# Smaller pieces for the quantising pass over three weights, two PSUM banks instead of four in the attention groups, and waits moved to the buffers now used

## The reference, cut to what matters

```
sa, ca, ga, sb, cb, gb = split(silu(c) @ wmod)            # ga, gb: at least 0.25 in size
h = layernorm(x) * (1 + ca) + sa
x = x + ga * attn_block(h)      # q, k, v, attention over the 16 heads of a token, o, gelu MLP 1024-4096-1024
h = layernorm(x) * (1 + cb) + sb
x = x + gb * ffn(h)

def weight_quant(w): s = 1 / clip(mean(|w|), 1e-5); return clip(round(w * s), -1, 1) / s
def act_quant(x):    s = 127 / clip(max(|x|, rows), 1e-5); return clip(round(x * s), -128, 127) / s
def bitlinear(x, w): return act_quant(x) @ weight_quant(w).T
def ffn(x): return bitlinear(silu(bitlinear(x, w_gate)) * bitlinear(x, w_up), w_down)
```

## Time and profile before

| | us |
|---|---|
| median of 2 runs | 8587.61 (8584.29 and 8590.92) |
| the profiled execution, its own time | 8546.85 |
| its span (first to last instruction, slowest core, core 7) | 8545.1 |
| spans of the 8 cores | 8489.9 to 8545.1 |
| outside the span in that execution | 1.75 |
| core 7, from the start to the first load of pass 1 | 412 |
| core 7, the three weights' preparation | 412 to 1037 |
| core 7, the eight chunks | 1037 to 8545 |

### The profile page before, as it was taken

The page is one execution under the profiler, slowest core; times in us unless marked ns, Lnnn a source line. Parts: engine busy times, 40 slices in busy tenths (PEclk is TensorE's granted clock), DMA queues, the critical chain, the costliest instruction groups (busy, mean ns, idle before and its releaser), DMA issues.

```text
span 8545.1 us, 71718 instructions; the slowest of 8 cores (8489.9 to 8545.1 us)
## 1 busy us (share of the span) xinstructions
PE 4842.0 (57%) x23948; PEld 2382.1 (28%) x23948; DVE 3130.7 (37%) x5728; ACT 1002.1 (12%) x2077; POOL 73.6 (1%) x109
## 2 busy tenths in 40 slices
PE   0700066666565575665666666656566656656566
PEld 0700033223322152223322242224322332224222
DVE  0033343253315432354325432543335331543244
ACT  0000011111111011101111111101110111111110
POOL 0011000000000000000000000000000000000000
PEclk9999966887688776886688767877788768867788
DMA  9555501333032311332033212341133203321133
GB/s 106 146 201 202 200 30 35 74 84 94 22 79 68 89 50 30 78 90 69 23 79 86 79 41 56 76 104 36 34 74 85 88 22 80 74 81 51 37 80 89
DMA packets 1033748, 667.50 MB, mean 78 GB/s; under 512 B 806192, under 2 KB 937392, under 8 KB 1017264
## 3 DMA queue, kind: packets, MB, share of 16 engines
q1 hardware_dynamic: 1018608, 537.09, 24.2%
q0 software_dynamic: 14784, 125.84, 6.1%
HBM read 646.09 MB, written 67.11 MB: 83 GB/s over the span
## 4 chain that ended last, share of the span: by engine, by line
PE 41%; DMA 23%; DVE 19%; issue 9%; ACT 5%; another core or an unknown queue 3%; DVEq 1%; ACTq 0%; SPq 0%; POOL 0%; POOLq 0%
PE pA L586 5%; PE pB L586 4%; PE pB L1066 4%; DMA wbigB<-scr_u 3%; DMA wbigB<-scr_fc 3%; DVE sbd L678 3%; PE pA L1060 3%; DVE vtmp L1150 2%; DMA wbigA<-scr_u 2%; PE pB L933 2%; DVE vtmp L489 2%; PE bcA L264 2%; DMA wbigB<-scr_g 2%; PE pA L933 2%
## 5 line engine op out<-in xcount | busy, mean ns | idle before, releaser
L942 DVE SCALAR_TENSOR_TENSOR vtmp<-pA,c_projb_f,afm 128x512 f32<-128x512 f32 x32 | 24.0, 751 | 1047.4 <-PE pA L933 1047.4
L439 PE MATMUL bcA<-amid,onescol_b 128*1 128x512 bf16 x256 | 99.3, 557 | 471.6 <-DVE amid L432 471.6
L1082 DVE TENSOR_TENSOR gu<-pB,gt 128x512 f32<-128x512 f32 x256 | 177.0, 692 | 453.7 <-PE pB L1066 453.7
L1060 PE MATMUL pA<-mmin,wbigB 128*128 128x512 bf16 x1024 | 258.0, 391 | 136.4 <-DMA wbigB<-scr_g 94.5
L1060 PE MATMUL pA<-mmin,wbigA 128*128 128x512 bf16 x1024 | 260.7, 394 | 117.6 <-DMA wbigA<-scr_g 73.6
L264 PE MATMUL bcA<-siluc,gfm 128*128 128x1 f32 x768 | 164.1, 352 | 247.7 <-DMA gfm<-wmod 247.7
L1066 PE MATMUL pB<-mmin,wbigB 128*128 128x512 bf16 x1024 | 253.5, 392 | 89.3 <-DMA wbigB<-scr_u 89.0
L1080 ACT ACTIVATE sig<-gt 128x512 bf16<-128x512 f32 x256 | 161.5, 631 | 1142.6 <-DVE gt L1077 1142.5
L1066 PE MATMUL pB<-mmin,wbigA 128*128 128x512 bf16 x1024 | 253.3, 392 | 58.0 <-DMA wbigA<-scr_u 57.3
L350 PE MATMUL bcB<-onecol_f,trA 128*1 128x1 f32 x6 | 0.6, 163 | 491.0 <-DVE prep_r L339 491.0
L586 PE MATMUL pA<-mmin,wbigA 128*64 128x256 bf16 x1536 | 225.3, 290 | 38.9 <-ACT mmin L499 38.9
(11 more groups left out here) (266 smaller groups left out, 8697.1 us busy)
## 6 DMA issues: line engine op xcount, KB each, us to landing
gfm<-gB POOLq DMA_DIRECT2D x32, 1024.0 KB, 6.2
gfm<-uB POOLq DMA_DIRECT2D x32, 1024.0 KB, 6.3
gfm<-dB POOLq DMA_DIRECT2D x32, 1024.0 KB, 6.2
wbigB<-scr_fc SPq DMA_DIRECT2D x128, 256.0 KB, 2.9
wbigA<-scr_fc SPq DMA_DIRECT2D x128, 256.0 KB, 2.9
wbigB<-scr_g SPq DMA_DIRECT2D x128, 256.0 KB, 2.9
wbigA<-scr_u SPq DMA_DIRECT2D x128, 256.0 KB, 2.8
wbigA<-scr_g SPq DMA_DIRECT2D x128, 256.0 KB, 2.9
```

Of the source, the lines that this page charges most:

```text
L1060: ev_mg = p.op("tensor", (lambda oc, kc, wbg_, slg: lambda t: t.matmul(out=pslot(slg), lhsT=wbg_[:, kc * 128:(kc + 1) * 128], rhs=mmin[:, ...
L1082: ev_p3 = p.op("vector", (lambda slu, gt, gu: lambda v: v.tensor_tensor(out=gu[:], in0=pslot(slu), in1=gt[:], op=ALU.mult))(slu, gt, gu), ...
```

## The change

Three things are changed.

1. Pass 2 of `prep_quant` works in pieces. Each tile is still loaded whole (1 MB, by POOL, two buffers). VectorE takes it in four pieces of 512 columns: piece h is multiplied and rounded into its own int32 buffer `prep_iv[h]` (trA, rsxg_t, sxb2_t, scaleb_t, which the chunks use later) and clipped into half of a bf16 buffer `prep_bv[h // 2]` (the two gt tensors). After pieces 1 and 3 SP stores 128 x 1024 bf16 (256 KB). The clip of a piece also waits for the last store from its buffer (`st_last`). The multiply waits for `evo`, which is reassigned at each store.
2. The attention's groups use midA and midB in turn (g mod 2) instead of four banks.
3. Since gfm's first half is no longer used by the preparation, Gelu's outputs 0 to 15 of chunk 0 no longer wait for the last store of the preparation, and 16 to 31 still do. The first users in chunk 0 of trA, rsxg_t, sxb2_t, scaleb_t and of the two gt tensors in the gate stage wait for that store.

```diff
@@ prep_quant, pass 2
-                evi = p.op("vector", (lambda buf, sw_col: lambda v: v.tensor_scalar(
-                    out=prep_i[:], in0=buf[:], scalar1=swb[:, sw_col:sw_col + 1],
-                    scalar2=None, op0=ALU.mult))(buf, sw_col),
-                    deps=(evd, ev_swb, evo), sig=True)
-                evc = p.op("vector", lambda v: v.tensor_scalar(
-                    out=prep_b[:], in0=prep_i[:], scalar1=1.0, scalar2=-1.0,
-                    op0=ALU.min, op1=ALU.max), deps=(evi,), sig=True)
-                evo = p.op("sync", (lambda r, c0: lambda s: s.dma_start(
-                    out=dst[128 * r:128 * (r + 1), c0:c0 + 2048], in_=prep_b[:]))(r, c0),
-                    deps=(evc,), dma="q")
+                for h in range(4):
+                    evi = p.op("vector", (lambda buf, sw_col, h: lambda v: v.tensor_scalar(
+                        out=prep_iv[h], in0=buf[:, 512 * h:512 * (h + 1)],
+                        scalar1=swb[:, sw_col:sw_col + 1],
+                        scalar2=None, op0=ALU.mult))(buf, sw_col, h),
+                        deps=(evd, ev_swb, evo), sig=True)
+                    evc = p.op("vector", (lambda h: lambda v: v.tensor_scalar(
+                        out=prep_bv[h // 2][:, 512 * (h % 2):512 * (h % 2) + 512],
+                        in0=prep_iv[h], scalar1=1.0, scalar2=-1.0,
+                        op0=ALU.min, op1=ALU.max))(h),
+                        deps=(evi, st_last[h // 2]), sig=True)
+                    if h % 2 == 1:
+                        evo = p.op("sync", (lambda r, c0, h: lambda s: s.dma_start(
+                            out=dst[128 * r:128 * (r + 1),
+                                    c0 + 1024 * (h // 2):c0 + 1024 * (h // 2) + 1024],
+                            in_=prep_bv[h // 2][:]))(r, c0, h),
+                            deps=(evc,), dma="q")
+                        st_last[h // 2] = evo
                 evq_hist.append(evo)
@@ attention, per group
-                mname = mname4[g % 4]
-                mb = midp4[g % 4]
-                vb = vst_ps4[g % 4]
+                mname = "mid%d" % (g % 2)
+                mb = midp[g % 2]
+                vb = vst_ps[g % 2]
@@ Gelu of chunk 0
-                deps=[ev_mm] + ev_const + ([prep_done["d"]] if ci == 0 else []), sig=True)
+                deps=[ev_mm] + ev_const +
+                ([prep_done["d"]] if (ci == 0 and oc >= 16) else []), sig=True)
```

More of the change, by code:

```diff
@@ L203, in build_nc @@
     prep_r = sb("prep_r", [128, 18])
+    prep_iv = [trA[:, :].bitcast(I32), rsxg_t[:, :].bitcast(I32),
+               sxb2_t[:, :].bitcast(I32), scaleb_t[:, :].bitcast(I32)]
+    prep_bv = [gtr[0][:, :].bitcast(BF16), gtr[1][:, :].bitcast(BF16)]
     pP = [psal("pA", [128, 1024]), psal("pB", [128, 1024])]
@@ L208, in build_nc @@
     vst_ps = [midp[0][:, 264:296].bitcast(BF16), midp[1][:, 264:296].bitcast(BF16)]
-    midp4 = None
     sems = {s: ctx.enter_context(nc.semaphore(s)) for s in
             ("sT", "sV", "sS", "sG", "sQ", "dq0", "dq1", "dg0", "dg1")}
-    midp4 = [midp[0], midp[1], bcp[0], bcp[1]]
-    vst_ps4 = [mb_[:, 264:296].bitcast(BF16) for mb_ in midp4]
-    mname4 = ["mid0", "mid1", "bc0", "bc1"]
     BT = {"bc0": [], "bc1": [], "mid0": [], "mid1": []}
@@ L371, in prep_quant @@
         evq_hist = []
+        st_last = [None, None]
         i = 0
@@ L978, in build_nc @@
                     out=trA[:], in0=hfm[:, 0:chunk], in1=hfm[:, chunk:2 * chunk],
-                    op=ALU.max), deps=[evs_h2[0], evs_h2[1], evs_h2[-1]] +
+                    op=ALU.max), deps=[evs_h2[0], evs_h2[1], evs_h2[-1],
+                                       prep_done["d"] if ci == 0 else None] +
                     ([("dq0", p.counts["dq0"]), ("dq1", p.counts["dq1"])] if DBG else []),
@@ L1011, in build_nc @@
             out=rsxg_t[:], in_=bcp[1][:, 0:chunk], func=AF.Identity),
-            deps=(ev_rgb,), sig=True)
+            deps=(ev_rgb, prep_done["d"] if ci == 0 else None), sig=True)
         bank_r("bc1", ev_rgt)
@@ L1076, in build_nc @@
                 dep_p1.append(ev_prod[-2])
+            if ci == 0 and oc < 2:
+                dep_p1.append(prep_done["d"])
             ev_p1 = p.op("vector", (lambda slg, gt: lambda v: v.tensor_tensor(
@@ L1124, in build_nc @@
             out=sxb2_t[:], in_=bcp[0][:, 0:chunk], func=AF.Identity),
-            deps=(ev_sxb2,), sig=True)
+            deps=(ev_sxb2, prep_done["d"] if ci == 0 else None), sig=True)
         bank_r("bc0", ev_sxt2)
@@ L1141, in build_nc @@
             out=scaleb_t[:], in_=bcp[1][:, 0:chunk], func=AF.Identity),
-            deps=(ev_scb,), sig=True)
+            deps=(ev_scb, prep_done["d"] if ci == 0 else None), sig=True)
         bank_r("bc1", ev_sct)
```

## The result

The changed kernel takes 8748.7 us (median of 11 runs), the kernel before 8586.62 (median of 10). The ratio is 1.0184, with a 95% interval from 1.0149 to 1.0218: 158 us or 1.8% slower, where 8730 and 1.7% were forecast. The ratio leaves out one run of the changed kernel in which the four cores of one die were slower at a lower clock. The profiled execution took 8725.05 us.

A forecast was written before the change was run, and what follows sets the result against it. Pass 2 of the weight preparation was seen as a ring waiting for stores; 42 longer rounds (124.7 us) plus first and last tiles made 142.7 us, so 8587.6 + 142.7 = 8730 us, range 8615 to 8800.

The forecast's parts named there:

- The ring: Pass 2 of the preparation: a round holds two stores in sequence, 11.11 us, 2.97 more than 8.14, in 42 rounds: 124.7 us.
- The stores: Pass 2: a tile's first store stands behind the load, 4.7 us; the second finds no load, 1.95 us.
- VectorE: Pass 2 pieces: multiply 486 ns, clip 427 ns, a half tile 2.05 us, a tile 4.10 where it was 2.62.
- The cover: Pass 2: VectorE's longer work counts in full in each round, 4.10 us a tile where it was 2.62.
- Banks and moved waits: Attention's two banks (1.97 us of slack) and Gelu's and chunk 0's moved waits: both costed at nothing.
- Rival 1: Pass 2: the first store gets out ahead of the load, both stores cost 1.95 us, 8615 us; chance 0.13.
- Rival 2: Pass 2: stores cost by number, not size, 5.3 and 2.65 us, a round of 12.41, 8793 us; chance 0.19.
- Rival 3: Pass 2: not slower; smaller stores slip past the load at 1.6 us each, round 7.66, 8577 us; chance 0.04.
- rival 4: Attention: a wait for the bank at each group, 51 us on top of the forecast, 8781 us; chance 0.02.

The follow-up runs named there:

- the two partial kernels: Changed kernel with old pass 2 put back: 0.998 of the kernel before; changed kernel with four attention banks again: 1.0196 of the kernel before.

## Why the prediction was right

- The ring. The step said that pass 2 is a ring of multiply, clip and store, and that the reassigned `evo` puts two stores into it. Taking away the wait of piece 2 alone gives back 153.2 of 154.1 us. Shown.
- The stores. The first behind the load was put at 4.7 us, with 5.17 if the load does not move forward. The rows give 233.5 us of waiting for 48 first stores; six of them (first and last tiles) wait about 2.2, which leaves 5.24 for each of the other 42, and less the hand-overs of 0.18 a landing of 5.06. The term was mis-sized by 0.36 us in 42 rounds, 15 us. The second was put at 1.95; 106.6 us over 45 waits (125.8 less 19.2 for loads) are 2.37, or 2.19 for the store, 11 us more over all rounds. In all VectorE waits 359 us ahead of its multiplies, for the 333 forecast.
- VectorE. 486 and 427 ns to the nanosecond (480 and 481 for the multiplies of pieces 1 and 3). A half tile takes 1.95 us and not 2.05, since the second multiply starts 0.1 us before the first clip's end (497.16 for 496.81 + 0.43): 0.1 us in each of 96 half tiles, some 10 us less. Together 142.7 + 15 + 11 - 10 = 159, beside 154 on average and 156 between the two cores whose rows are used (1193.3 on core 3 now, 1037.1 on core 7 before). The errors partly cancel.
- The cover. I let VectorE's extra time count in full, 1.5 us a round. With one store a tile it would not have counted at all; the four pieces alone are even faster than the whole tile. In the changed kernel the first half's work is hidden as well: the first store lands 7.1 us into the round, where half of the old store's data would have landed at 7.3. The loss is what stands behind that landing: the second half tile, 1.95 us, its store, 2.2, and two hand-overs. Much of the 0.36 us above is this same thing, counted from the store's issue.
- Banks and moved waits at nothing. Shown by the two partial kernels; the groups of the attention start 2.4 to 2.8 us apart before and now.
- Rival 1 (the first store gets out ahead) did not come about, and its reasoning was wrong as well: it compared the bulk of the load's data, 3.0 us into the round, with the store's at 2.85. The row itself has the load's first data at 2.0 to 2.2 us and full flow from 3.2, and the kernel with the load after the multiply shows that a thin flow between them is of no use to a store issued behind the load. The load's issue, 0.45 us into the round, is always ahead of a store at 2.03. The rule of the Trainium skill that I leaned this rival on (SBUF — State Buffer, Who interferes with whom: the two engines block each other) agrees with POOL's rows, an issue of 527 ns alone and 690 now, but the load never came late enough. Rival 2 (cost by number) is refuted as the cause: the second store takes 2.2 us and not 2.65, and with the wait of piece 2 gone the number of stores costs 25 us. Rival 3 did not come about, and rival 4 is refuted by the partial kernels.

## What to carry to other kernels

Before splitting a transfer into smaller ones, look at what the producer waits for: an event variable that is reassigned inside the new loop made each half wait for the other, and the overlap that the second buffer allows was never used. Where one transfer sets the length of a ring, see whose turn it is in the DMA queues. A prefetch whose issue began 0.9 us ahead of the store on the critical path made that store 4 us longer (6.7 for 2.7), and letting the load wait for the clip, in place of the store's landing, bought 101 us in one line. Also look at which operation a wait protects: the store reads what the clip writes, so it is the clip that has to wait for it, and not the multiply.

## What the runs showed of the hardware that I had not expected

- A store of SP that was issued while POOL was still issuing a load moved nothing for 3.2 us, although hardly anything flowed in 0.9 of them; then both flowed beside each other for about 1.6 us. Issued 0.5 us ahead of the load it landed in 2.7 us. What holds it is not shown.
- The load's own length is not the same in all kernels, at the same 1 MB. Median of pass 2, from issue to landing: 5.2 us with no store beside it, 5.5 in four pieces with one store (issued 3.9 us into the round), 6.0 in the changed kernel (a store at 2.0), 6.2 with the wait at piece 0 alone (stores at 2.0 and 3.9), 6.3 in the kernel before (a store at 2.7), 6.8 with the load after the multiply, and 6.2 and 5.6 in the two kernels with the load after the clip (whole tiles and pieces). The faster load goes with the gain of one late store of 512 KB over two of 256 KB, 25 us in all. What sets it, the time of the store's issue, the number of stores or POOL's own issue, was not separated.
- POOL's issue of a load takes 527 ns alone, 957 beside a multiply of 1286 ns, 897 beside a clip of 1227, and 690 beside a multiply and a clip of 486 and 427, each time ending about 0.1 us behind the end of one of them.
